# A state-space layer on one core: the MLP of a batch moved into the scans of the next, x rows parked in DRAM

## What is computed

```python
def step(hst, inp):                      # 512 steps, for each of 8 batches, in both directions
    dt_t, B_t, C_t, x_t = inp
    dA = jnp.exp(dt_t[:, :, None] * A)
    hst = hst * dA + dt_t[:, :, None] * B_t[:, None, :] * x_t[:, :, None]
    y = jnp.einsum('bdn,bn->bd', hst, C_t)          # 512 channels, 32 states
    return (hst, y)
...
x = x + g1[:, None, :] * (fwd + bwd)     # fwd, bwd: the scan's y + Dp * x, times silu(z), projected
h = _ln(x, norm2_w, norm2_b)
h = h * (1.0 + s2[:, None, :]) + sh2[:, None, :]
mlp = _silu(h @ w1) * (h @ w2) @ w3      # 256 -> 384 -> 256
return x + g2[:, None, :] * mlp
```

## Time and profile before

| | us |
|---|---|
| median of three runs | 5845.6 |
| lowest, highest | 5844.1, 5849.22 |
| the profiled execution, its own time | 5844.69 |
| its span, to which the rows below refer | 5842.8 |

### The profile page before, as it was taken

How to read it: one execution, slowest core, us unless ns; L and a number is a source line. 1 busy time by engine, 2 the same in 40 slices (tenths; PEclk the granted TensorE clock), 3 DMA queues, 4 the chain that set the end, 5 groups by cost and what they waited for, 6 DMA issues and landing times. The chain is left out here.

```text
span 5842.8 us, 74727 instructions
## 1 busy us (share of the span) xinstructions
PE 5511.4 (94%) x27336; PEld 2865.9 (49%) x27336; DVE 4311.1 (74%) x5020; ACT 4113.3 (70%) x6785; POOL 2804.3 (48%) x2191
## 2 busy tenths in 40 slices
PE   8999999999999997999998999999999999999998
PEld 5444445555555554444444444444544445454445
DVE  6767744444444444776867989899898999989898
ACT  3555454554444543555558989899998989989897
POOL 0000012232222321010106969699696978969697
PEclk8999999999999998999999999999999999999999
DMA  5342420000000004233223020110202012020200
GB/s 145 47 66 34 83 30 3 1 3 3 2 3 1 3 2 63 48 62 63 48 45 69 30 54 30 42 43 24 59 30 54 30 29 56 26 58 30 54 30 22
DMA packets 171934, 222.33 MB, mean 38 GB/s; under 512 B 40881, under 2 KB 107274, under 8 KB 171314
## 3 DMA queue, kind: packets, MB, share of 16 engines
q1 hardware_dynamic: 171570, 217.56, 17.1%
HBM read 152.90 MB, written 30.49 MB: 31 GB/s over the span
## 5 line engine op out<-in xcount | busy, mean ns | idle before, releaser
L2480 DVE TENSOR_TENSOR_SCAN l__h<-l__decay,psum 128x1024 f32<-128x1024 f32 x1024 | 2249.6, 2267 | 55.9 <-ACT l__decay L1928 15.5
L2446 POOL TENSOR_TENSOR l__hc<-l__h,l__c_rep 128x1024 f32<-128x1024 f32 x1016 | 2012.4, 2013 | 92.5 <-DMA l__c_rep<-l__c_dram 46.5
L1928 ACT ACTIVATE l__decay<-l__dt_rep,l__a_neg 128x511 f32<-128x511 f32 x2048 | 1339.6, 708 | 9.6 <-DVE l__h L2480 9.3
L1938 PEld LDWEIGHTS psum<-ident,l__dtx_B 128*128 128x128 f32 x8192 | 882.7, 141 | 850.9 <-DVE l__h L2480 496.1
L2564 PE MATMUL psum<-l__hc,l__gather 128*64 128x512 f32 x4096 | 1105.2, 618 | 139.8 <-POOL l__hc L2446 139.3
L1938 PE MATMUL psum<-ident,l__dtx_B 128*128 128x128 f32 x8192 | 1119.3, 280 | 35.6 <-DVE l__h L2480 16.8
L1912 ACT ACTIVATE l__dtx_B<-l__dtx_T,l__b_T 128x512 f32<-128x512 f32 x1664 | 1103.4, 709 | 5.5 <-PE psum L1938 3.4
L683 DVE TENSOR_REDUCE l__row_max<-psum 128x1 f32<-128x512 f32 x1024 | 648.7, 680 | 207.4 <-PE psum L717 203.8
L1367 POOL TENSOR_SCALAR l__probs<-l__probs,l__rec 128x512 f32<-128x512 f32 x512 | 348.6, 694 | 886.4 <-DVE l__rec L1363 886.4
L199 POOL TENSOR_SCALAR l__ln_var_eps<-l__ln_mean_var 128x4 f32<-128x4 f32 x56 | 16.1, 287 | 1433.6 <-DVE l__ln_mean_var L185 1433.6
L1040 ACT ACTIVATE l__probs<-psum 128x1024 f32<-128x1024 f32 x512 | 501.9, 1023 | 147.5 <-PE psum L1101 141.2
(11 more groups left out here) (184 smaller groups left out, 6193.9 us busy)
## 6 DMA issues: line engine op xcount, KB each, us to landing
l__c_rep<-l__c_dram SPq DMA_DIRECT2D x512, 128.0 KB, 2.8
l__dt_rep<-l__dt SPq DMA_DIRECT2D x128, 256.0 KB, 5.0
l__parts_dram<-l__parts SPq DMA_DIRECT2D x64, 384.0 KB, 3.5
l__q_stack<-l__parts_dram SPq DMA_DIRECT2D x192, 128.0 KB, 6.5
l__k_stack<-l__parts_dram SPq DMA_DIRECT2D x192, 128.0 KB, 9.1
l__w<-in_l_w SPq DMA_DIRECT2D x6, 1024.0 KB, 6.3
l__gate_rows<-l__gates_dram SPq DMA_DIRECT2D x24, 256.0 KB, 3.2
in_mod_w<-in_mod_w SPq DMA_DIRECT2D x1, 4608.0 KB, 17.8
```

The costliest lines, as they stand in the source:

```text
L1928: nc.scalar.activation(decay[:, i % DECAYS, s, 1:T], dt_rep[:, w, c, s, 1:T], ACT.Exp, scale=a_neg[:, g, c, s:s + 1]).then_inc(S["decay"], 1)
L1938: last = nc.tensor.transpose(bx_psum(i)[:, s, t * P:(t + 1) * P], dtx_B[:, (k + 1) % 2, t, 2 * c + s, :, :].rearrange("p j d -> p (j d)"), ...
L2446: nc.gpsimd.tensor_tensor(hc[:, i % HCS, :, :], h[:, i % HS, :, :], c_of(i), ALU.mult).then_inc(S["hc"], 1)
L2480: nc.vector.tensor_tensor_scan(both(h[:, i % HS, :, :]), both(decay[:, i % DECAYS, :, :]), both(bx_psum(i)), 0.0, ALU.mult, ALU.add).then_ ...
```

## The change

- **x rows.** Only two batches of x stay in the first two slots of `x_sb` (KEPT = 2, batch b in slot b % 2). The third layer stores batches 2 to 7 to DRAM as they are finished (`spill`); in the stage of batch b (1 to 6) the fourth layer's SP, at group 3, stores batch b - 1 to the output, waits until that has landed, and loads batch b + 1 into the same slot, before the gate rows and `c_rep` of group 3. The last spill stands ahead of `first_sync`.
- **The free slots of `x_sb`** hold three more `hc` buffers (HCS = 7), `hT_mlp` with `mlp_tmp`, and `hid`, which the profile will name `x_sb`.
- **The MLP.** Of its six up-projection halves two stand in the gap among the transposes, one ahead of and one behind the two first fills, and the last two in units 1 and 2; the down projection is spread over units 3 to 5 (`mlp_step`). silu(a) is made as 0.5·a·(1 + tanh(a/2)): a tanh on ACT (`tanh_up`), two instructions on DVE (`mlp_products`), of which those for blocks 1 and 2 stand after scans 1 and 3. The scaling is after scans 5 and 7, POOL's additions before units 8 and 9. Both adds still precede the store.
- **Sums.** After the first batch, `y_sum` stands 7 units behind, and from unit 48 on catches up by one every 8 units until it is 2 behind.
- **The gap.** The first block of the convolution stands between the gates; `project_in` 4 to 7 stand in a row ahead of `project_x`; evictions are divided anew between ACT and DVE (DVE takes `hT_mlp`, `b_T` and half of `dtx_T`, and scales five of the first group's pieces of `dtx_B`, `scale_first`); the first decay stands ahead of the last transposes. SP's two stores of C wait for both halves.

The core of the diff:

```diff
@@ mamba_layer
-    DECAYS, HS, HCS, CS = 3, 3, 4, 4
+    DECAYS, HS, HCS, CS = 3, 3, 7, 4
+    VEC_OPS = 5
-    RESIDUAL_AFTER, STORE_AT, ROWS_FIRST_AT = (1, 2), 3, 10
+    RESIDUAL_AFTER, ADD_AT, STORE_AT, ROWS_FIRST_AT = (5, 7), (8, 9), 3, 10
+    BEHIND, CATCH_UP = 7, 40
...
@@ narrow_attention_layer, sync_batch
+                    if spill and b > KEPT:
+                        spill(sp, b - 1)
...
+            if spill and not more:
+                sp.wait_ge(*S.at("res", 2 * 2 * RES_STEPS))
+                spill(sp, b)
             if F:
                 sp.wait_ge(*S.at("oT", NG))
                 F.sync(sp)
...
@@ between_vector
-            if begin and end:
-                convolve(dve)
+            if begin and end:
+                gate(0)
+                gate(1)
+                convolve(dve, range(1))
+                gate(2)
+                gate(3)
+                convolve(dve, range(1, IC))
...
@@ between_tensor
-                project_in(pe, IC)
-                project_in(pe, IC + 1)
-                for c in range(IC):
-                    project_x(c)
-                project_in(pe, IC + 2)
-                project_in(pe, IC + 3)
-                project_dt(0)
+            for c in range(IC):
+                project_in(pe, IC + c)
+            for c in range(IC):
+                project_x(c)
+            if end:
+                pe.wait_ge(*S.at("res", 2 * 2))
+                norm.tensor(nc, pe, 1, bank[4:6])
+            project_dt(0)
+            project_dt(1)
...
+        def mlp_products(dve, j, behind):
+            dve.wait_ge(*S.at("tanh", j + 1 - behind))
+            nc.vector.scalar_tensor_tensor(hid[:, j, :], hid[:, j, :], 1.0, bank[UP_BANKS[j][0]],
+                                           ALU.add, ALU.mult).then_inc(S["silu"], 1)
+            dve.wait_ge(*S.at("silu", j + 1 - behind))
+            nc.vector.scalar_tensor_tensor(hid[:, j, :], hid[:, j, :], 0.5, bank[UP_BANKS[j][1]],
+                                           ALU.mult, ALU.mult).then_inc(S["prod"], 1)
...
@@ sync_batch
                 if k == STORE_AT and b:
                     sp.wait_ge(*S.at("mlp_add", 0))
                     store(sp, b - 1)
+                    if begin:
+                        sp.wait_ge(s_out, 16 * b)
+                        sp.dma_start(x_slot(b + 1), x_dram[b + 1]).then_inc(s_x_in, 16)
...
@@ gpsimd_batch
-                if i in (HCS - 2, HCS - 1) and S.batch:
+                if i in ADD_AT and S.batch:
...
@@ tensor_batch
+                if S.batch:
+                    mlp_step(pe, i)
-                if i >= 2:
-                    y_sum(i - 2)
+                behind = max(2, BEHIND - max(0, i - CATCH_UP) // 8) if S.batch else 2
+                while summed <= i - behind:
+                    y_sum(summed)
+                    summed += 1
```

More of the change, by code:

```diff
@@ new lines, in between_scalar @@
+            silu_x(0)
+            silu_x(1)
+            y_first(0)
+            silu_x(2)
+            y_first(1)
+            silu_z(0)
+            silu_z(1)
+            silu_x(3)
+            y_first(2)
+            silu_z(2)
+            y_first(3)
+            silu_z(3)
+            for w in range(2):
+                act.wait_ge(*S.at("dc_filled", w + 1))
+                nc.scalar.activation(dc[:, w, :], bank[DC_BANKS[w]][0:ROWS, :], ACT.Copy).then_inc(S["dc"], 1)
+            for c in range(IC):
+                softplus(c)
@@ new lines, in between_scalar @@
+            take_forward(0)
+            take_forward(1)
+            if not end:
+                negative_a(act)
+            first_decay(act, 0, nxt)
+            take_forward(2)
+            take_forward(3)
+            if end:
+                tanh_up(act, 0, 0)
+            act.wait_ge(*S.at("c_out", 32))
+            act.wait_ge(*S.at("bT", 1))
+            act.wait_ge(*S.at("dtxT_fwd", IC))
+            for q in range(IC):
+                scale_pair(q)
+            for i in range(1, DECAYED):
+                first_decay(act, i, nxt)
@@ new lines, in between_tensor, with up_half @@
+            first_fill(0)
+            pe.wait_ge(*S.at("dtxT_fwd", IC))
+            pe.wait_ge(*S.at("dtxT_back", IC))
+            first_fill(1)
+            if end:
+                up_half(pe, 1, 1).then_inc(S["up_filled"], 1)
+        def up_half(pe, j, k):
+            for c in range(DC):
+                last = nc.tensor.matmul(bank[UP_BANKS[j][k]], (w1, w2)[k][:, c, j * P:(j + 1) * P], hT_mlp[:, c, :],
+                                        start=(c == 0), stop=(c == DC - 1))
+            return last
@@ L2530, in scalar_batch @@
             for i in range(UNITS):
+                if i in (1, 3) and S.batch:
+                    tanh_up(act, (i + 1) // 2, HC)
                 if i + DECAYED < UNITS:
```

365 lines of the change are left out of this document (182 added, 183 removed).

## The result

The changed kernel takes 5858.7 us (median of 9 runs, 5858.2 to 5866.6) against 5844.1 us (median of 9, 5840.5 to 5849.2): the ratio is 1.0027, with a 95% interval of 1.0018 to 1.0036. It is slower by 15 us, a little more than can be told from no change. The forecast was 5847, with a range of 5822 to 5866 and a chance of 0.25 for slower.

A forecast was written before the change was run, and what follows sets the result against it. The prediction took POOL's chain from product 0 to bound the stage and the transfers to bound product 0. The terms -3.0 + 7.8 - 2.0 = +2.8 us took 5844.7 to 5847, range 5822 to 5866.

The forecast's parts named there:

- POOL as the limit: In the stage: once started POOL never waits, so its chain from product 0 sets the last scan; each wait counts.
- Product 0 bound by the transfers: In the gap: product 0 comes 22.1 us after softplus 0, at t = 58.3, 3.1 us earlier than before.
- Rivals B: In the gap: scan 0, not the transfers, binds product 0, 5 us less in 7 gaps, 5811; chance 0.05.
- D: In the gap: no shortening, softplus 0 stays at t = 37.4; +1.2 x 7, 5855; chance 0.08.
- The waits ahead of products 5 to 7: Early in the stage: POOL waits 1.1 + 0.4 = 1.5 us ahead of products 6 and 7, bounds 0 and 4.
- rival C: Units 3 to 6: PE falls behind; at 4 us of POOL's wait instead of 1.5, +18, 5865; chance 0.18.
- The wait for group 3's `c_rep`: Ahead of product 12: POOL waits 3.7 us in stages 1 to 6, bounds 1.6 to 5.5; 0.4 in stage 7.
- Rival A: At group 3: the wait for `c_rep` hardly arises, 3.7 x 6 = 22 us less, 5825; chance 0.22.
- The end of the stage: Last scan at p = 287.0, directly when product 124 is done; 4.4 us later than before's 282.6.
- The layer's start: Fourth layer's start: product 0 at 3116.4 instead of 3118.5, its stage's end 0.9 earlier still; -3.0 us.
- The spills: Third layer: storing 512 KB six times while the queue is idle costs nothing.
- The sum: Whole kernel: -3.0 at the start, +7.8 for stages 1 to 6, -2.0 for stage 7; +2.8 us.

The follow-up runs named there:

- Experiment 6: The changed kernel with group 0's `c_rep` loaded ahead of the last four `dt_rep` transfers and a batch's first three products in free x slots: 5831.7 us.
- experiment 4: The changed kernel with 12 useless matmuls added behind unit 2's piece of the MLP, so that PE does not idle ahead of fill 4: 5848.3 us.
- Experiment 2: The changed kernel with only the wait for the store and the reload of x moved ahead of group 6's `c_rep`: 5840.8 us.
- Experiments 1: The changed kernel with store, reload of x and gate rows ahead of group 6's `c_rep` instead of group 3's: 5842.2 us.
- the runs with two and three edits: The changed kernel with the edits of experiments 1 and 3 together, 5818.5 us, and with that of Experiment 6 as well, 5818.7 us.
- experiments 1 and 3: 1 as above; 3 is the changed kernel with POOL's two scalings for group 1 made ahead of product 0: 5834.5 us.

## Why the forecast came out as it did

The two waits, the queue ahead of product 0 and POOL as the limit were laid out rightly, and the time lies in the range. But the sum gave +2.8 us where the profiled execution has +13.5, 10.7 short, and what costs most, the fall of PE's clock, stands nowhere in it. Step by step:

- **Product 0 bound by the transfers: right.** Softplus 0 at t = 36.0 (forecast 36.2), product 0 at 57.8 in the mean (58.3). Experiment 6 shows that the queue held it. Rivals B and D fall.
- **The waits ahead of products 5 to 7: mis-sized.** The forecast had 1.5 us, bounds 0 to 4; it is 3.05 in the mean with the sum's 0.24. The order of work was as laid out, but the term took full-speed durations from rows in which PE had been busy, while PE now idled 5.5 us ahead of fill 4. The clock fell, and fill 4 and four pieces cost 1.7 us more in the stage shown (1.94 + 2.66 against 1.04 + 1.88). At full speed the term would have been too large, not too small: 0.9 us with the sum's 0.24 in experiment 4. So the clock's share is 2.1 us a stage in the mean of stages 1 to 6. As rival C has it, PE falls behind in these units, at 1.55 us of its 2.5 over the forecast, but for a reason that C doesn't name; some 12 us over seven stages. Experiment 4 gives 10 back.
- **The wait for group 3's `c_rep`: right in kind, too large.** 3.7 us forecast, 2.1 measured, with 0.5 of small waits behind it. The landing was 0.3 quicker and the chain behind the load 1.5; POOL itself got there 1 us later. Experiment 2 shows the chain as its cause. Rival A falls: the wait is there in stages 1 to 6 (and not in 7).
- **The end of the stage: a step that failed.** I let the last scan follow product 124 at once and so took 0.8 us from each stage. It doesn't. DVE waits for POOL ahead of scan 124, for 0.16 us, and the three scans behind it follow at DVE's own pace of 2.2 us, where POOL's products take 1.96: so the last scan starts 0.8 us behind product 124's end (4089.23 to 4090.05), about as before. I had named POOL alone as the limit; to the last three scans it is DVE. Experiments 1 and 2 bear out that POOL's waits count in full from where the changed kernel stands, and the runs with two and three edits show the next limit 6 us a period further on, at DVE's first scans.
- **The layer's start: -3.0 forecast, -1.0 measured.** From residual to product 0 it is 1.9 us less (41.9 to 40.0), near the 2.1 of the forecast. But the third layer's residual came 0.7 us later; that difference arises in layers the change hardly touches and is within what they vary by. And the 0.9 us more that I gave the end of stage 0 is missing, for the reason above: from product 0 to the end it took 282.3, before 282.2. The spills as such can't be told from nothing.
- **The sum.** 6 stages at +1.1 over forecast (0.45 of waits, 1.1 for the end, of which 0.8 is the step above and 0.3 stays unexplained, less 0.5 in the gap), 6.5 us; stage 7 at +2.3 (its waits for scans were 3.8 instead of 1.5 and 0.4, and the end again); the start 2.0. Together 10.7, but for rounding. The 0.45 is small by luck: 1.55 too little for the scans, 1.6 too much for group 3's `c_rep`, and 0.5 of small waits. With that `c_rep` term right the sum would have been some 10 us lower, and further off.

Where the expected gain went: the gap's 3.6 us were bought with a stage in which POOL first waits for fills at half clock and then for a queue with a reload in it. Of the 7.9 us by which scan 0 is now ahead of product 0, experiment 6 used 3.8 a gap, and nothing once experiments 1 and 3 had taken the waits away.
